# A two-layer graph attention kernel: one store, one reduction and one copy issued at other places of each step

## What is computed

```python
# layer 0: 8 heads of 64
Q, K, V = x @ W_q + b_q, x @ W_k + b_k, x @ W_v + b_v
scores = einsum('bihd,bjhd->bhij', Q, K) / sqrt(64)
scores = scores + (x @ w_g[:512])[:, :, None] + (x @ w_g[512:])[:, None, :] + b_g + log(adj + 1e-9)
x = einsum('bhij,bjhd->bihd', softmax(scores), V) + x
# layer 1: one head, masked by adj == 0
scores = einsum('bod,bid->boi', x @ Wq + bq, x @ Wk + bk) / sqrt(512)
attn = softmax(where(adj == 0, -1e18, scores)), with masked entries set to 0
x = x + einsum('boi,bie->boe', attn, x) @ Wc
out = layernorm(x) * gamma + beta
```

## Time and profile before

| | us |
|---|---|
| median of 3 runs | 2360.61 |
| the runs | 2357.82 to 2362.62 |
| the profiled execution, its own time | 2356.35 |
| its span, first to last instruction | 2354.6 |
| PE, busy share of the span | 96% |
| DVE, ACT, POOL | 79%, 53%, 39% |
| mean granted TensorE clock | 0.989 |

### The profile page before, as it was taken

How to read it: one execution, slowest core, us unless ns; L and a number is a source line. 1 busy time by engine, 2 the same in 40 slices (tenths; PEclk the granted TensorE clock), 3 DMA queues, 4 the chain that set the end, 5 groups by cost and what they waited for, 6 DMA issues and landing times.

```text
span 2354.6 us, 39731 instructions
## 1 busy us (share of the span) xinstructions
PE 2259.9 (96%) x13256; PEld 1872.5 (80%) x13256; DVE 1856.3 (79%) x5371; ACT 1240.2 (53%) x3492; POOL 906.8 (39%) x1139
## 2 busy tenths in 40 slices
PE   9999999999999999999999999999999999999998
PEld 6877788777887878877788877778777787777886
DVE  6687788777878787887788877877778778778886
ACT  6555555455554445555455545555455554555554
POOL 2144243443443433444424344334343343442443
PEclk9999999999999999999999999999999999999999
DMA  6333333333333343333333343333333333333332
GB/s 220 113 120 123 123 111 104 121 126 121 109 116 116 114 130 118 110 110 118 120 122 114 103 125 126 125 116 110 108 117 126 117 108 117 111 128 121 111 103 71
DMA packets 204061, 277.82 MB, mean 118 GB/s; under 512 B 26064, under 2 KB 128208, under 8 KB 203728
## 3 DMA queue, kind: packets, MB, share of 16 engines
q1 hardware_dynamic: 203568, 274.75, 36.5%
q10 hardware_dynamic: 288, 0.52, 0.1%
HBM read 166.34 MB, written 108.85 MB: 117 GB/s over the span
## 4 chain that ended last, share of the span: by engine, by line
PE 41%; DVE 24%; POOL 12%; issue 10%; DMA 8%; ACT 3%; SPq 2%; DVEq 0%
PE bank L244 11%; PE bank L245 11%; PE bank L246 11%; DVE x1n L1210 8%; POOL probs L1510 8%; DMA turn_dram<-turned 7%; DVE probs L1120 7%; PE bank L548 5%; POOL x_lo L1518 4%; DVE x_lo L1153 3%; ACT att L873 2%; SPq L275 2%; PE bank L535 2%; DVE att L1252 1%; DVE nmax L1120 1%
## 5 line engine op out<-in xcount | busy, mean ns | idle before, releaser
L1510 POOL TENSOR_TENSOR probs<-probs,rcp 128x512 f32<-128x512 f32 x256 | 275.8, 1098 | 792.2 <-DVE rcp L1130 792.0
L828 ACT ACTIVATE probs<-probs,nmax 128x128 f32<-128x128 f32 x1024 | 397.5, 392 | 36.0 <-DVE nmax L1120 36.0
L1210 DVE STREAM_TRANSPOSE x1n<-xT_land 32x512 f32<-32x512 f32 x496 | 348.5, 703 | 9.9
L244 PE MATMUL bank<-x_hi,wk_hi 128*128 128x512 f32 x512 | 215.3, 420 | 82.6 <-POOL x_lo L1518 82.4
L1139 DVE STREAM_TRANSPOSE turned<-probs 128x1024 f32<-128x1024 f32 x128 | 159.4, 1246 | 148.0 <-DMA turn_dram<-turned 85.4
L1518 POOL TENSOR_TENSOR x_lo<-xT_land,x_hi 128x512 fp32r<-128x512 f32 x124 | 165.4, 1356 | 241.0 <-ACT x_hi L778 241.0
L1120 DVE CUSTOM_DVE_ANT_0 probs<-bank,ln_adj 128x128 f32<-128x128 f32 x1024 | 227.1, 287 | 4.1
L244 PEld LDWEIGHTS bank<-x_hi,wk_hi 128*128 128x128 f32 x512 | 98.5, 192 | 137.8 <-POOL x_lo L1518 120.9
L246 PE MATMUL bank<-x_hi,wk_lo 128*128 128x512 f32 x512 | 206.4, 403 | 0.0
L245 PE MATMUL bank<-x_lo,wk_hi 128*128 128x512 f32 x512 | 206.1, 403 | 0.0
L244 PE MATMUL bank<-wc_hi,x_hi 128*128 128x512 f32 x512 | 203.2, 397 | 0.0
(11 more groups left out here) (154 smaller groups left out, 5199.9 us busy)
## 6 DMA issues: line engine op xcount, KB each, us to landing
turn_dram<-turned SPq DMA_DIRECT2D x128, 512.0 KB, 2.9
probsT<-turn_dram SPq DMA_DIRECT2D x512, 128.0 KB, 2.7
xT_land<-in_xT SPq DMA_DIRECT2D x126, 256.0 KB, 4.2
xn<-in_x SPq DMA_DIRECT2D x126, 256.0 KB, 3.9
out<-x1n SPq DMA_DIRECT2D x124, 256.0 KB, 2.0
adj_sb<-in_adj SPq DMA_DIRECT2D x32, 256.0 KB, 3.0
c_rows<-c_dram SPq DMA_DIRECT2D x31, 256.0 KB, 4.3
at_dram<-scratch SPq DMA_DIRECT2D x31, 256.0 KB, 2.3
```

Source lines behind the costliest of these rows:

```text
L244: nc.tensor.matmul(out_ap, st[0], mv[0], start=start, stop=False)
L828: op = nc.scalar.activation(probs[:, k, :], probs[:, k, :], ACT.Exp, bias=nmax[:, k:k + 1], scale=-1.0, accum_out=sums[:, k:k + 1])
L1210: op = nc.vector.transpose(x1n[b * BLK:(b + 1) * BLK, :, :] .rearrange("p g (c a s) -> p a c g s", c=C, a=P // BLK)[:, a, :, :, :], x1_lan ...
L1510: nc.gpsimd.tensor_tensor(probs[:, half, :], probs[:, half, :], rcp[:, half].unsqueeze(2).to_broadcast([P, HALF, P]), ALU.mult)\
```

## The change

It moves instructions and adds or removes none.

- SP, steps 1 to 30: `move_probs` is cut into `store_probs` and `fetch_probs`. For pair 2 the store is issued before the four `load_x`, the fetch after them.
- ACT, steps 1 to 30: `next_x_high(t, 1)` is issued before `exp1(u)`.
- DVE, `layer1_begin`, steps 1 to 31: `masked_scores(u)` is issued before `turn(t, 3)`.
- DVE, `final_step`: `residual0(t, 0)` is issued before `turn_attention(u)` and `residual0(t, 1)` right after it, both ahead of `factors1(u)` and `y_low(u, 0)`.

```diff
-            def move_probs(t, c):
+            def store_probs(t, c):
 
                 sp.wait_ge(s["dve_t"], nth("dve_t", t, c))
...
                 sp.dma_start(turn_dram[c], turned[:, :, :, :].rearrange("p b k s -> p (b k s)"))\
                     .then_inc(s_pw[c], 16)
+
+            def fetch_probs(t, c):
+
                 sp.wait_ge(s_pw[c], 16 * (t + 1))
...
+            def move_probs(t, c):
+                store_probs(t, c)
+                fetch_probs(t, c)
@@ sync, step
                     move_probs(t, c)
+                store_probs(t, 2)
                 for d in range(C):
...
                     load_x(t + 1, d)
-                move_probs(t, 2)
+                fetch_probs(t, 2)
                 load_xn(t + 1, 2)
@@ scalar, step
                 y_out(u, 0)
-                next_x_high(t, 0)
+                for d in range(2):
+                    next_x_high(t, d)
                 exp1(u)
-                for d in range(1, C):
+                for d in range(2, C):
                     next_x_high(t, d)
@@ vector, layer1_begin
                 row_term(u, 3)
+                masked_scores(u)
                 turn(t, 3)
-                masked_scores(u)
@@ vector, final_step
                 layer1_begin(t)
+                residual0(t, 0)
                 turn_attention(u)
+                residual0(t, 1)
                 factors1(u)
                 y_low(u, 0)
-                residual0(t, 0)
-                residual0(t, 1)
                 y_low(u, 1)
```

## The result

| | before | changed |
|---|---|---|
| median, us | 2361.61 (4 runs, 2357.82 to 2364.89) | 2231.85 (4 runs, 2231.25 to 2232.46) |
| profiled execution, own time | 2356.35 | 2232.46 |
| span | 2354.6 | 2230.7 |
| mean granted clock | 0.989 | 0.999 |

The ratio is 0.9451, with a 95% interval of 0.9435 to 0.9467: 5.5% faster. The forecast was 2259 with 2250 to 2290 around it. The sign and the mechanism came out as forecast; the size did not.

A forecast was written before the change was run, and what follows sets the result against it. PE bounds the kernel, stalled once per step for `x_lo`; 30 steps of 69.2 us in place of 2177.6 give 101.6, less 3.6 is 98: 2356.35 becomes 2258.3, plus 0.7 is 2259 us, range 2250 to 2290.

The forecast's parts named there:

- The bound and the chain: PE is the bound, interrupted once per step at the first projection waiting for `x_lo`, 82.4 us in all.
- The length of a step without the stall: PE's own work in a step: 71.8 us less 2.6 us of wait, 69.2 us; 30 steps make 2076.
- The 3.6 us left for the first step and late loads: Taken off the 101.6 us gain for the first step's other waits and a few late loads, leaving 98.
- The range: Forecast's own range 2250 to 2268, chance 0.78; reaching up to 2290 to leave out no more than 2 in 10.
- The clock: Granted clock stays 1.00 from step 2 to step 30; its falls no longer touch PE.
- the 101.6: Gain over 30 steps if each takes 69.2 us: 2177.6 - 2076 us.
- The median over the profiled execution: Median of the runs was 4.3 us above the profiled execution; only 0.7 us added for the changed kernel.
- Blocking against POOL: Rival: DVE's masked operations take 4.0 us in place of 1.09 beside POOL's `x_lo`; 2298 us, chance 0.04.
- Late loads ahead of `exp1`: Rival: loads land late in most steps, chunk 1 before `exp1` costs 0.5 to 1 us; 2275 to 2290, chance 0.06.
- The context products: PE has 2.2 us to spare for `att1T_low`; rival that the stall moves there: 2274 us, chance 0.06.
- The final step: PE's 0.63 us wait for `residual0` goes, context products may wait 0.8 us; taken as nothing, plus or minus 1.5.

The follow-up runs named there:

- e8: Kernel before with chunk 0's three products made three times more in each step, its three waits kept: 2349.66 us, ratio 0.9961.
- e7: Changed kernel with the SP part undone, the store of pair 2 again behind the x loads: 2253.78 us, ratio 0.9544.
- e9: Kernel before with one edit on ACT, all four copies of x ahead of `exp1`: 2273.86 us, ratio 0.9622.
- e4: Kernel before with PE's three projection waits made one and chunk 0's three products made three times more: 2434.16 us, ratio 1.0308.
- e1: Kernel before with only the DVE part of the steps, masked scores ahead of `turn(t, 3)`: 2264.02 us, ratio 0.9586.
- e5: Changed kernel with the ACT part undone, chunk 1 copied behind `exp1` again: 2232.62 us, ratio 0.9463.

## Why the prediction was right and wrong

- **The bound and the chain** were right: PE, one stall in each step, and behind it `x_lo`, `x_hi`, `exp1`, the masked scores, `turn(t, 3)`, the store. Every link moved, and to within 0.5 us of the time laid out. The reading that this stall is the one thing between PE and its own work was right too.
- **The length of a step without the stall** was the step that failed: 69.2 in place of 68.35. I subtracted the idle time in brackets, though the front part said that starts tell how long PE is taken. 30 x 0.85 = 25.5 us of the 27 by which the forecast was off. The 3.6 us left for the first step and late loads were right (2.5 and 0.9). The range missed it too: it allowed for less gain than the sum and hardly for more, as if the brackets could not be short. Its low end of 2250 is 9 us under the forecast, and the terms named for it make 5. On the high side stand 5 us for late loads, a sum that no run shows: the one late step of 2 to 30 cost 0.95.
- **The clock** was right in kind: no fall in steps 2 to 30, a granted clock of 1.00 in each. In the sum it had no term of its own; it lay in the 101.6, as what the wait leaves over of a mean step, 3.4 - 2.75, which is 20 us in all. No run shows 20 us for the clock; e8 puts its falls at 9 us net.
- **The median over the profiled execution**: I took 0.7 of the 4.3 us. The changed kernel's median lies 0.6 under its profiled execution, and its runs spread over 1.2 us in place of 7. That they would draw together was right; the 1.3 us between 0.7 and -0.6 are the rest of the miss.
- **Blocking against POOL** did not occur: 345 ns for a masked operation in the mean, 334 before.
- **Late loads ahead of `exp1`** did occur, once in steps 2 to 30, with 7.1 us to landing where I had found 5.9. Both are medians of a step's four loads; the load of chunk 1 alone took 6.7 and 5.8. This is ACT in the step from 1799.10:

```profile
1835.28 0.63 ACT L786 ACTIVATE x_hi<-xT_land 128x512 fp32r<-128x512 f32 x1 [2.82 <-DMA xT_land<-in_xT]
1835.93 1.28 ACT L881 ACT_TABLE_LOAD   x1
1837.22 0.40 ACT L881 ACTIVATE att<-att,stats 128x128 f32<-128x128 f32 x1
```

  That step took 69.30, 0.95 more than the others, though PE's waits show 0.28 in it, before chunk 3. The break before chunk 2 was too short to stand among the waits:

```profile
1840.37 0.39 PE L246 MATMUL bank<-x_hi,wk_lo 128*128 128x512 f32 x1
1840.83 0.50 PE L244 MATMUL bank<-x_hi,wk_hi 128*128 128x512 f32 x1
```

  Its starts are 0.46 us apart in place of 0.23. The exponentials start at 1837.22, right at the end of the table load (1835.93 + 1.28).
- **The context products** had 2.2 us of slack in the prediction. `att1T_low` ended at 46.1 us after the first scores, as laid out, and at up to 47.4 in other steps, against 48.3 when PE wants it; e7 and e9 show what that slack was worth.
- **The final step** was taken at nothing and cost 0.3, which is within the scatter of its order (table above).

## What to carry to other kernels

Before a gap on PE is priced, take the starts on both sides of it and subtract the starts of the same stretch where it runs unbroken: the idle time shown was too small by the same piece, 0.28 us, for each break here, and short breaks hid as much as they showed or stood in no list at all. Where two or three chains end at the same engine just in time, find the link that they share and move that one; edits that lengthen slack don't add up. A copy that is needed early should not stand behind work of another chain, but the reverse holds too: put it ahead only where what it waits for is surely there.

## What I had not expected of the hardware

A break costs PE 0.28 us beyond what the profile shows, nearly the same in three kernels, one with three breaks in a step (before, 0.84 for the three) and two with one (e4 and e9, 0.29 in the steps read). A kernel that did 61 us of needless products during the stall was 9 us faster (0.9961, 0.9947 to 0.9975). A fall of the clock cost 1.6 us where nothing behind it had slack (e4) and about half of that where short waits followed: 9 us over the 12 steps that it touched. Single breaks of 2.3 to 4.0 us brought the fall in 26 of 29 steps, where breaks of 1.8 to 3.5 with two short ones behind brought it in 12. And POOL took 4.2 to 4.8 us for three chunks of `x_lo` where the gate, an operation of DVE with two inputs in SBUF, ran at the same time (e1), and 3.8 where it was all but through before them (e5).
